# The small work of the two expert stages in more pieces at other steps, and x of the last two edges normalised by ScalarE instead of GpSimd

## The reference, cut to what matters

```python
def _layernorm(x, axis=-1, eps=1e-05):
    m = jnp.mean(x, axis=axis, keepdims=True)
    v = jnp.var(x, axis=axis, keepdims=True)
    return (x - m) / jnp.sqrt(v + eps)
...
    x = x + _layernorm(_L2_ffn_ref(_layernorm(x, axis=-1), ...), axis=-1)    # stage 5
    x = x + _layernorm(_L3_attn_ref(_layernorm(x, axis=-1), ...), axis=-1)   # stage 6
    x = x + _layernorm(_L3_ffn_ref(_layernorm(x, axis=-1), ...), axis=-1)    # stage 7
    return x
```

## Time and profile before

| | |
|---|---|
| time, median of 3 runs | 1632.12 us (1631.22 to 1632.94) |
| time of the profiled execution | 1629.69 us |
| its span | 1627.9 us, 22138 instructions |
| busy, PE | 1288.8 us (79%) |
| busy, VectorE (DVE) | 1079.5 us (66%) |
| busy, ScalarE (ACT) | 1140.7 us (70%) |
| busy, GpSimd (POOL) | 271.1 us (17%) |
| granted TensorE clock, mean over the span | 0.877 of full speed |
| expert stage 5 | from about 1110 to 1384 us of the span |
| expert stage 7 | from about 1384 to 1628 us |

### The profile page before, as it was taken

One profiled execution on the slowest core, in us unless ns is written; L12 is line 12 of the kernel. 1 busy time (PEld: TensorE's weight loads), 2 busy tenths in 40 slices (PEclk: granted clock), 3 DMA queues, 4 the chain that ended last, 5 costly groups with the idle time before them and its releaser, 6 DMA issues.

```text
span 1627.9 us, 22138 instructions
## 1 busy us (share of the span) xinstructions
PE 1288.8 (79%) x8028; PEld 659.5 (41%) x8028; DVE 1079.5 (66%) x2031; ACT 1140.7 (70%) x1619; POOL 271.1 (17%) x361
## 2 busy tenths in 40 slices
PE   5598888876676777777777777678988988887996
PEld 2233333344011111111111144456767776665875
DVE  6877877054455664566456655556978679767898
ACT  3166777755999999999999834345555645876985
POOL 4500003042000000000000034083011034803000
PEclk9589999997688788878877899888999998999998
DMA  5611020002410000101000030002323225011111
GB/s 178 154 22 22 23 41 3 2 1 87 107 20 0 20 17 4 20 0 20 20 1 1 1 151 1 1 1 66 106 83 93 88 73 171 27 33 33 47 44 54
DMA packets 40765, 74.65 MB, mean 46 GB/s; under 512 B 6096, under 2 KB 10448, under 8 KB 39888
## 3 DMA queue, kind: packets, MB, share of 16 engines
q1 hardware_dynamic: 39792, 71.67, 15.6%
q10 hardware_dynamic: 864, 1.57, 0.3%
HBM read 59.26 MB, written 13.96 MB: 45 GB/s over the span
## 4 chain that ended last, share of the span: by engine, by line
PE 38%; ACT 24%; DVE 19%; issue 12%; POOL 4%; DMA 2%; SPq 0%; POOLq 0%; DVEq 0%; ACTq 0%
ACT SHARED L1035 15%; PE PS L823 4%; PE PS L992 4%; PE PS L979 3%; DVE NM L732 3%; DVE SHARED L1045 3%; PE PS L712 2%; PE PS L645 2%; PE PS L1762 2%; PE PS L787 2%; PE PS L1764 2%; PE PS L1763 2%; DVE KS L1917 2%; PE PS L1215 2%; PE PS L1771 2%
## 5 line engine op out<-in xcount | busy, mean ns | idle before, releaser
L1035 ACT ACTIVATE SHARED<-PS 128x1536 f32<-128x1536 f32 (+1 forms) x352 | 466.1, 1437 | 31.2 <-PE PS L979 30.2
L979 PE MATMUL PS<-QS,KS 51*128 51x512 bf16 (+1 forms) x1024 | 242.0, 461 | 134.1 <-ACT SHARED L1035 128.7
L1045 DVE TENSOR_TENSOR SHARED<-SHARED 128x1536 f32<-128x1536 f32 (+1 forms) x176 | 286.6, 1703 | 86.4 <-ACT SHARED L1035 86.4
L803 ACT ACTIVATE SHARED<-PS 128x512 f32<-128x512 f32 (+3 forms) x384 | 164.4, 494 | 96.6 <-PE PS L791 87.3
L979 PEld LDWEIGHTS PS<-QS,KS 51*128 51x128 bf16 (+1 forms) x1024 | 41.2, 99 | 386.8 <-ACT SHARED L1035 358.6
L992 PE MATMUL PS<-SHARED,Vg 128*16 128x512 f32 x1024 | 157.9, 694 | 1.7 <-DVE SHARED L1045 1.6
L732 DVE TENSOR_REDUCE NM<-PS 128x2 f32<-128x1024 f32 (+3 forms) x128 | 129.0, 1022 | 28.5 <-PE PS L718 20.4
L1762 PE MATMUL PS<-ROUNDED 128*128 128x512 f32 x328 | 138.8, 423 | 4.9 <-ACT KS L1863 4.2
L1763 PE MATMUL PS<-ROUNDED 128*128 128x512 f32 x328 | 132.5, 404 | 0.0
L1764 PE MATMUL PS<-ROUNDED 128*128 128x512 f32 x328 | 132.3, 403 | 0.0
L1851 ACT ACTIVATE ROUNDED<-KS 128x512 fp32r<-128x512 f32 x100 | 63.0, 630 | 82.8 <-DVE KS L1917 82.8
(11 more groups left out here) (265 smaller groups left out, 2314.4 us busy)
## 6 DMA issues: line engine op xcount, KB each, us to landing
SHARED<-wx SPq DMA_DIRECT2D x64, 256.0 KB, 3.1
qx<-SHARED SPq DMA_DIRECT2D x24, 256.0 KB, 4.0
SHARED<-in_moe SPq DMA_DIRECT2D x3, 1600.0 KB, 11.9
kx<-SHARED SPq DMA_DIRECT2D x18, 256.0 KB, 4.0
SHARED<-wx SPq DMA_DIRECT2D x16, 224.0 KB, 3.0
SHARED<-qx SPq DMA_DIRECT2D x16, 192.0 KB, 4.7
SHARED<-kx SPq DMA_DIRECT2D x16, 192.0 KB, 5.3
QS<-qx SPq DMA_DIRECT2D x16, 192.0 KB, 4.5
```

The costliest lines, as they stand in the source:

```text
L803: act.activation(PB[t % 3][:, h, q0:CH], bank(RING0[n % 3], q0), ACT.Exp, scale=SCORE_SCALE)\
L979: ins = pe.matmul(bank((v % 2) * GRP + f - a), KS[g % 2][r, h // 2, kt * P:kt * P + P], QS[g % 2][r, h // 2, qh * CH:(qh + 1) * CH], start ...
L1035: act.activation(dst, PS[:, (v % 2) * GRP * CH:((v % 2) * GRP + b - a) * CH], ACT.Exp if second == qh else ACT.Sigmoid, scale=SCORE_SCALE)\
L1045: dve.tensor_tensor(ex_tile(j), ex_tile(j), GR[w % RING][:, 0:(b - a) * CH], ALU.mult)\
```

## The change

Four things are edited. `dve_x` is cut into `dve_x_sum` and `dve_x_stats`, the routing functions of both stages are cut into more pieces (`dve_route5_b2`, `dve_route5_c2`, `dve_route7_b2`), nearly all small pieces stand at other steps on all three engines, and edges 6 and 7 lose `pool_apply`, so that ScalarE writes XN, in `act_apply` calls at steps of their own.

```diff
         def dve_x(dve, own, e, c):
+            dve_x_sum(dve, own, e, c)
+            dve_x_stats(dve, own, e, c)
+
+        def dve_x_sum(dve, own, e, c):
             if e.norm_y:
                 dve.wait_ge(y_root, e.n_y(c))
                 for t in tiles(c):
                     ins = dve.scalar_tensor_tensor(out=tile(X, t), in0=e.y_tile(t), scalar=RSY[:, e.slot, t:t + 1],
                                                    in1=tile(X, t), op0=ALU.mult, op1=ALU.add)
                 ins.then_inc(x_sum, 1)
-                dve.wait_ge(x_sum, e.n_y(c))
...
+        def dve_x_stats(dve, own, e, c):
+            if e.norm_y:
+                dve.wait_ge(x_sum, e.n_y(c))
             if e.turn:
                 dve_stats(dve, own, STX, MVX, lambda t: tile(e.stream(), t), c).then_inc(x_var, 1)
...
-            own.link(dve.tensor_reduce(out=best[:, :, 7:8], in_=sel, axis=AX.X, op=ALU.add))
+            own.mark(dve.tensor_reduce(out=best[:, :, 7:8], in_=sel, axis=AX.X, op=ALU.add))
+
+        def dve_top_k_ties(dve, own, vals, e, k, sel, best, tmp, nt=NT):
+
+            a, b, c = tmp
+            own.wait()
             own.link(dve.tensor_scalar(best[:, :, 7:8], best[:, :, 7:8], -1.0, float(k), ALU.mult, ALU.add))
...
@@ pe_beside_moe5
-            if c and r == (9 if c == 3 else 4):
+            if c and r == (12 if c == 3 else 4):
...
                 pe_turn_y(pe, edges[6], c - 1, OT5, A[5, "ot"], c)
-            if c and r == (17 if c == 3 else 9):
+            if c and r == (19 if c == 3 else 11):
                 pe_turn_x(pe, edges[6], c - 1)
-            if c in (1, 2) and r == 11:
+            if c in (1, 2) and r == 13:
                 pe_lin_features(pe, c - 1, 0)
-            if c in (1, 2) and r == 15:
+            if c in (1, 2) and r == 16:
                 pe_lin_features(pe, c - 1, 1)
-            if c == 2 and r == 18:
+            if c == 2 and r == 19:
                 pe_lin_kv(pe, 0)
-            if c == 2 and r == 20:
+            if c == 2 and r == 21:
                 pe_lin_out(pe, 0)
-            if c == 2 and r == 23:
+            if c == 2 and r == 24:
                 pe_lin_proj(pe, 0)
-            if c == 3 and r == 4:
+            if c == 3 and r == 6:
                 pe_turn_x(pe, edges[7], 0)
-            if c == 3 and r == 5:
+            if c == 3 and r == 8:
                 pe_turn_x(pe, edges[7], 1)
...
@@ act_beside_moe5
             if c and r == (18 if c == 3 else 10):
+                act_apply(act, edges[6], c - 1)
+            if c and r == (20 if c == 3 else 12):
                 act_turned(act, edges[6], c - 1)
-            if c in (1, 2) and r == 12:
+            if c in (1, 2) and r == 14:
                 act_lin_features(act, c - 1, 0)
-            if c in (1, 2) and r == 16:
+            if c in (1, 2) and r == 17:
                 act_lin_features(act, c - 1, 1)
...
             if c == 3 and r == 5:
+                act_apply(act, edges[7], 0)
+            if c == 3 and r == 6:
+                act_apply(act, edges[7], 1)
+            if c == 3 and r == 7:
                 act_turned(act, edges[7], 0)
-            if c == 3 and r == 6:
+            if c == 3 and r == 8:
                 act_turned(act, edges[7], 1)
-            if c == 3 and r == 10:
+            if c == 3 and r == 13:
                 act_route7(act, 0, 0)
-            if c == 3 and r == 12:
+            if c == 3 and r == 17:
                 act_route7(act, 0, 1)
...
@@ dve_beside_moe5
-            if c == 0 and r == 8:
+            if c == 0 and r == 7:
                 dve_route5_b(dve, own, 1)
-            if c == 0 and r == 12:
+            if c == 0 and r == 10:
+                dve_route5_b2(dve, own, 1)
+            if c == 0 and r == 13:
                 dve_route5_c(dve, own, 1)
             if c == 0 and r == 16:
+                dve_route5_c2(dve, own, 1)
+            if c == 0 and r == 19:
                 dve_route5_d(dve, own, 1)
-            if c and r == (10 if c == 3 else 5):
+            if c and r == (13 if c == 3 else 5):
                 dve_y(dve, own, edges[6], c - 1)
-            if c and r == (12 if c == 3 else 6):
-                dve_x(dve, own, edges[6], c - 1)
-            if c in (1, 2) and r == 13:
+            if c and r == (15 if c == 3 else 7):
+                dve_x_sum(dve, own, edges[6], c - 1)
+            if c and r == (16 if c == 3 else 8):
+                dve_x_stats(dve, own, edges[6], c - 1)
+            if c in (1, 2) and r == 15:
                 dve_lin_features(dve, c - 1, 0)
-            if c in (1, 2) and r == 16:
+            if c in (1, 2) and r == 18:
                 dve_lin_features(dve, c - 1, 1)
-            if c == 2 and r == 18:
+            if c == 2 and r == 20:
                 dve_lin_kv(dve, 0)
-            if c == 2 and r == 24:
+            if c == 3 and r == 0:
                 dve_y(dve, own, edges[7], 0)
+            if c == 3 and r == 1:
                 dve_y(dve, own, edges[7], 1)
-            if c == 3 and r == 0:
-                dve_x(dve, own, edges[7], 0)
-            if c == 3 and r == 1:
-                dve_x(dve, own, edges[7], 1)
-            if c == 3 and r == 8:
+            if c == 3 and r == 2:
+                dve_x_sum(dve, own, edges[7], 0)
+            if c == 3 and r == 3:
+                dve_x_stats(dve, own, edges[7], 0)
+                dve_x_sum(dve, own, edges[7], 1)
+            if c == 3 and r == 4:
+                dve_x_stats(dve, own, edges[7], 1)
+            if c == 3 and r == 11:
                 dve_logits7(dve, 0)
                 dve_logits7(dve, 1)
-            if c == 3 and r == 9:
+            if c == 3 and r == 12:
                 dve_route7_a(dve, own, 0)
-            if c == 3 and r == 11:
+            if c == 3 and r == 14:
                 dve_route7_b(dve, own, 0)
-            if c == 3 and r == 13:
+            if c == 3 and r == 17:
+                dve_route7_b2(dve, own, 0)
+            if c == 3 and r == 18:
                 dve_route7_c(dve, own, 0)
...
@@ pe_beside_moe7
-            if c == 0 and m == 9:
+            if c == 0 and m == 8:
                 pe_lin_features(pe, 2, 1)
-            if c == 0 and m == 10:
+            if c == 0 and m == 11:
                 pe.wait_ge(A[6, "vf"], 5)
                 pe_turn_x(pe, edges[6], 3)
-            if c == 0 and m == 14:
+            if c == 0 and m == 15:
                 pe_lin_features(pe, 3, 0)
...
-            if c == 1 and m == 9:
+            if c == 1 and m == 11:
                 pe_turn_x(pe, edges[7], 2)
-            if c == 1 and m == 10:
+            if c == 1 and m == 13:
                 pe_turn_x(pe, edges[7], 3)
...
@@ act_beside_moe7
+            if c == 0 and m == 9:
+                act_lin_features(act, 2, 1)
             if c == 0 and m == 10:
-                act_lin_features(act, 2, 1)
-            if c == 0 and m == 11:
+                act_apply(act, edges[6], 3)
+            if c == 0 and m == 12:
                 act_turned(act, edges[6], 3)
...
-            if c == 1 and m == 10:
+            if c == 1 and m == 9:
+                act_apply(act, edges[7], 2)
+            if c == 1 and m == 11:
+                act_apply(act, edges[7], 3)
+            if c == 1 and m == 12:
                 act_turned(act, edges[7], 2)
-            if c == 1 and m == 11:
+            if c == 1 and m == 14:
                 act_turned(act, edges[7], 3)
...
@@ dve_beside_moe7
             if c == 1 and m == 1:
                 dve_y(dve, own, edges[7], 2)
+            if c == 1 and m == 2:
                 dve_y(dve, own, edges[7], 3)
-            if c == 1 and m == 3:
-                dve_x(dve, own, edges[7], 2)
+            if c == 1 and m == 4:
+                dve_x_sum(dve, own, edges[7], 2)
             if c == 1 and m == 5:
-                dve_x(dve, own, edges[7], 3)
+                dve_x_stats(dve, own, edges[7], 2)
+            if c == 1 and m == 6:
+                dve_x_sum(dve, own, edges[7], 3)
+            if c == 1 and m == 7:
+                dve_x_stats(dve, own, edges[7], 3)
...
-            if c == 1 and m == 19:
+            if c == 1 and m == 22:
                 dve_route7_b(dve, own, 1)
             if c == 1 and m == 24:
+                dve_route7_b2(dve, own, 1)
+            if c == 1 and m == 28:
                 dve_route7_c(dve, own, 1)
...
             if c == 2 and m == 18:
-                dve_x(dve, own, edges["end"], 0)
+                dve_x_sum(dve, own, edges["end"], 0)
+            if c == 2 and m == 19:
+                dve_x_stats(dve, own, edges["end"], 0)
                 dve_shift(dve, own, 0)
...
@@ edges
-                 6: Edge(6, 5, y_ready, y_at=(6, 6, 6, 6), t_at=(7, 7, 7, 7), pool_apply=True),
-                 7: Edge(7, 6, y_ready, y_at=(6, 7, 6, 7), t_at=(6, 7, 6, 7), split=True, pool_apply=True),
+                 6: Edge(6, 5, y_ready, y_at=(6, 6, 6, 6), t_at=(7, 7, 7, 7)),
```

(41 more changed lines are left out.)

34 lines of the change are left out of this document (18 added, 16 removed).

## The result

The changed kernel takes 1636.3 us (median of 20 runs, 1632.6 to 1643.9), the kernel before, beside it on the same chips, 1631.1 us (20 runs). The ratio is 1.0041, with a 95% interval of 1.0026 to 1.0055: slower by 0.4%. The means of the two lie 6.7 us apart, which is what the ratio says, and the medians 5.2. Run again beside other kernels it gave 1.0038 (1.0019 to 1.0057). The profiled execution has a span of 1634.5 us.

The account below looks back on a forecast made before the run. It took PE, busiest in nearly every chunk, and its waits (about 44 us not worked in five chunks) as the bound. Terms summed to -0.2 us on the profiled 1629.7 us, 2.4 us under the median, giving 1631.9 us; range 1622 to 1641.

Parts of the forecast that it names:

- Routing of stage 5 in pieces: Stage 5, chunk 0: smaller routing pieces fit in VectorE's gaps and allow three more steps of catching up, -0.5 us.
- Turning x and the kv sum: Stage 5, chunks 1 and 2: later turns shorten PE's waits for x, -4.8 us; PE waits before kv, +6.0 us.
- Chunk 3: Stage 5: earlier output copy gains, but the second exp waits for VectorE's routing piece in its own step, +1.0 us.
- Stage 7, chunk 0: ScalarE normalises edge 6's last x behind a features block, so PE waits 6 us at step 11, +4.0 us.
- Stage 7, chunk 1: Shorter waits for edge 7's x, fewer slow matmuls behind them, routing in two pieces: -5.5 us, bounds -9 and -3.
- End edge: x_stats only waits there and the shift moves one step; two delays shrink by some 0.2 us, -0.4 us.
- the slower one: Kv sum stands before its operands, exp of step 17 costs its whole 2.1 us: 1638.5 us, chance 30%.
- the rival's two signs: The slower rival decides once the kv wait is over about 7.5 us, or stage 7's gain under 2 us.
- The faster rival: Freed waits count and new ones don't; kv's wait and slow matmuls behind shorter waits go: 1624 us, chance 34%.
- GpSimd had blocked VectorE: Taking six normalisations from GpSimd shortens VectorE's chain by 2.3 us each, -14 us: 1618 us, chance 3%.

Follow-up runs that it names:

- the earlier activation: Changed kernel, but ScalarE normalises edge 6's last x at step 4 of stage 7 instead of step 10: ratio 1.0037 to the kernel before.
- The kernels with one stage new: Changed kernel with one stage's steps and GpSimd normalising as before: ratio 1.0013 with only stage 5 new, 1.0048 with only stage 7 new.
- the four edits: Changed kernel with routing 7's weights turned later, features' piece in ScalarE's step, second exp behind the normalisation, edge 6's last x normalised early: 1623.4 us, ratio 0.9970.
- the last four: Four edits with GpSimd normalising 0.9989, with stage 5's last turn two steps later 0.9988, without the features' piece edit 1.0006; changed kernel again 1.0038.

## Why the prediction was wrong

It forecast no change (-0.2 us) and got +6.7; the range held the time, but the gains and losses that were to cancel didn't. Its terms, against the two profiles of the changed kernel, whose chunks add up to 8.4 and 7.9 us more than before's:

- **Routing of stage 5 in pieces, -0.5:** -0.7 and -0.5. Right.
- **Turning x and the kv sum, chunks 1 and 2, -4.8 and +6.0 with +0.5 for chunk 1:** together +1.7 forecast, -0.4 and -0.5 measured. The waits came nearly as worked out (2.36 and 2.34 us for 2.7; 5.07 for 5.5), and the experiments put the kv wait at 3.7 us by the chunks and 5.9 by the ratios, for 6.0. Right in mechanism, 2 us off in size.
- **Chunk 3, +1.0:** +3.6 and +1.0. The waits grew by 2.3 and 2.7 us. The term had the exp's wait for VectorE's piece of the same step, and VectorE's idle time behind it came out as placed (2.23 us for 2.1), but it charged the wait to VectorE alone. Queued behind that exp was the normalisation that PE needed at step 19. With the exp behind it, PE's wait fell by 3.8 us, though the chunk hardly did; this chunk scatters too much (1.0 to 4.4 us over before in six profiles) to fault the size of the term.
- **Stage 7, chunk 0, +4.0:** +5.4 and +7.1. The wait was placed rightly and 7.3 us for 6; the chunk's slow matmuls were 9 and 14 more than before. Mis-sized by 1.4 to 3.1 us: the earlier activation gives 3 to 5 us back.
- **Stage 7, chunk 1, -5.5:** +0.7 and +0.7. This is the step that failed, with 6.2 us of the 6.9 us miss; the misses of the other terms cancel nearly. Its parts: the waits for x fell from 4.3 us to 1.8, as forecast (2.4), though as one wait and not two. Slow matmuls gave 1 to 2 us back, not 3 (before it was 13, not 15, that stood behind the two waits). Routing in two pieces gave nothing: one wait of 3.3 us became three of 1.0, 1.4 and 1.0. And the turning of the weights, which the prediction never followed, costs 3.4 us. I had looked at when the weights are sent out ("10 steps in hand") and not at how far their producer had moved: it went from VectorE's step 24 to 28, its reader from 28 to 30, so the distance fell from four steps to two. With the turning at step 2 of chunk 2 the chunk took 59.1 us, 4.7 less than with it at step 30 and 4.0 less than before, inside that term's bounds. So this one turning accounts for 4.7 of the 6.2 us.
- **End edge, -0.4:** the waits of chunks 2 and 3 fell by 1.0 us, but the stretch took 101.7 and 102.0 us for 101.9: nothing that can be told.

Of the rivals, the slower one (1638.5 us) has the right side but not the right cause. It put the loss on kv and on the exp. The kernels with one stage new showed that stage 5 as a whole costs about 2 us, which can't be told from nothing, and stage 7 carries the rest. Still, kv alone costs 4 to 6 us; the turns of x, which gain as forecast, pay for it. One of the rival's two signs, a gain in stage 7's chunk 1 under 2 us, did come, for a reason that it didn't name; the other, a kv wait over 7.5 us, did not. The faster rival fell since the new waits came and cost what the table of the four edits shows. That GpSimd had blocked VectorE during the normalisation fell too: with GpSimd normalising and otherwise the same steps the time is 3 to 6 us longer, not 14, the 3 being within the uncertainty, and PE's waits for the later x grow by 2.5 us in chunks 1 and 2 alone.

## What to carry to other kernels

When small work is moved in hand-ordered queues, list each handover as a pair (producer's step, reader's step) before and after, and cost every pair whose distance shrinks, including those whose reader isn't in the part that you are thinking of: three of the four here cost 3.7 to 4.8 us each. An operation that may wait for another engine must not stand ahead of one that has its input already; here ScalarE's 1.6 us of normalising, twice behind such a block, had PE wait for 6.4 and 7.3 us. A wait tells where to look and not what the place costs: take the length of the stretch with and without it, over a stretch long enough to come out the same twice. Where an edit has winning and losing handovers, mend the losing ones before judging it: four moved steps turned 0.4% slower into 0.3% faster.

## What the runs showed of the hardware

**Which clock follows a wait is not fixed by the program.** Two executions of the same kernel; the first matmuls behind the same wait in chunk 1. In one:

```profile
1196.35 0.66 PE L404 MATMUL PS<-ident,XN 128*128 128x128 f32 x4 [2.36 <-ACT XN L369]
...
1198.23 0.39 PE L1787 MATMUL PS<-ROUNDED 128*128 128x512 f32 x1
1198.46 0.39 PE L1788 MATMUL PS<-ROUNDED 128*128 128x512 f32 x1
```

In the other:

```profile
1199.54 0.66 PE L404 MATMUL PS<-ident,XN 128*128 128x128 f32 x4 [2.34 <-ACT XN L369]
...
1201.93 0.63 PE L1787 MATMUL PS<-ROUNDED 128*128 128x512 f32 x1
1202.35 0.63 PE L1788 MATMUL PS<-ROUNDED 128*128 128x512 f32 x1
```

Starts 0.23 us apart are the level of 2.4 GHz, 0.42 us that of 1.2 GHz; the granted clock of the 5 us from the first such start is 1.00 in the one execution and 0.77 in the other. One execution has 1 slow matmul in this chunk, the other 16, at 0.2 us each. The fast one then waits 1.37 us early in chunk 2 and has 7 slow matmuls there, the other 1, and by the end of chunk 2 both have taken the same time (136.5 and 136.4 us). In the changed kernel's 12 runs beside the last four, the time goes with the mean granted clock (correlation -0.95): 1633.0 us at 0.878, 1646.0 at 0.867, 1.1 us for each 0.001. So one profile's chunk is good to 3 us, its waits over 2 us to 0.05, and these two chunks together to 0.1. A difference of a few us between two kernels has to be read from waits and from stretches that repeat, and confirmed by many runs.

**VectorE and GpSimd do hold each other up, elsewhere.** In chunk 0 of stage 7 of the changed kernel, while GpSimd splits weights:

```profile
1403.60 1.07 POOL L1748 CAST ROUNDED<-SHARED 128x512 fp32r<-128x512 f32 x1
...
1405.14 1.77 DVE L1509 SCALAR_TENSOR_TENSOR XH<-Vg 128x512 f32<-128x512 f32 x1
...
1407.58 1.75 DVE L2298 TENSOR_TENSOR ROUNDED<-KS,ROUNDED 128x512 fp32r<-128x512 f32 x1
...
1411.08 0.61 POOL L1748 CAST ROUNDED<-SHARED 128x512 fp32r<-128x512 f32 x1
1411.12 0.62 ACT L2222 ACTIVATE ROUNDED<-SHARED 128x512 fp32r<-128x512 f32 x1
...
1411.77 0.69 DVE L2298 TENSOR_TENSOR ROUNDED<-SHARED,ROUNDED 128x512 fp32r<-128x512 f32 x1 [2.44 <-ACT ROUNDED L2222]
1411.78 1.81 POOL L1750 TENSOR_TENSOR ROUNDED<-SHARED,ROUNDED 128x512 fp32r<-128x512 f32 x1
```

The same subtraction of VectorE takes 0.69 or 1.75 us, the same cast of GpSimd 0.61 or 1.07. In the last two rows VectorE starts 0.01 us ahead of GpSimd and keeps its 0.69 us; GpSimd's own subtraction takes 1.81 us there and 1.26 at 1409.88, with VectorE idle. By the Trainium skill (SBUF — State Buffer, "Who interferes with whom") such operations of the two engines exclude each other; here the trace agrees, in that the operation that starts second is the longer one, while beside the normalisation of the earlier trace rows VectorE lost only 0.08 us. The prediction weighed the rule by that one row and not for this chunk. It did not decide the result, since the kernel before has the same slow operations here (1.78 us at L1502, 1.76 at L2249).
